# One kernel, one change: undivided softmax weights go through the turn, and the product with the values is divided by VectorE

## The reference, cut to what matters

```python
keys = modulated_linear(x, s, ...)      # [batch, position, 256]
# 16 heads of 16 features; for each batch and position the 16 heads attend to each other
w = softmax(q @ k.T * 16 ** -0.5)       # over the 16 heads j
o = w @ v                               # product with the values
x = x + modulated_linear(o, s, ...)
```

## Time and profile before

| | |
|---|---|
| median of 3 runs | 538.26 us (537.77 to 538.40) |
| span of the profiled execution | 537.6 us; its own time is not given apart, the median lies 0.7 us above the span |
| PE matmuls busy | 462.3 us, 86% |
| VectorE busy | 347.5 us, 65% |
| ScalarE busy | 282.6 us, 53% |
| GpSimd busy | 170.1 us, 32% |
| mean granted TensorE clock | 0.926 |
| chain that ended last | PE 67%, VectorE 14%, issue 5%, DMA 5%, SP queue 4%, ScalarE 3%, GpSimd 2% |

### The profile page before, as it was taken

How to read it: one execution, slowest core, us unless ns; L and a number is a source line. 1 busy time by engine, 2 the same in 40 slices (tenths; PEclk the granted TensorE clock), 3 DMA queues, 4 the chain that set the end, 5 groups by cost and what they waited for, 6 DMA issues and landing times.

```text
span 537.6 us, 9360 instructions
## 1 busy us (share of the span) xinstructions
PE 462.3 (86%) x3768; PEld 259.2 (48%) x3768; DVE 347.5 (65%) x653; ACT 282.6 (53%) x421; POOL 170.1 (32%) x146
## 2 busy tenths in 40 slices
PE   3896668924899999999999999999999898849981
PEld 3673335512365546554555654565546555424431
DVE  0374547593387488749856983898388778454923
ACT  0201488262853976578756966793976497102100
POOL 3009895110304232413231323314231420172121
PEclk9998767986599999999999999999999999879986
DMA  5991700331733713553183338143713561320011
GB/s 152 341 265 57 193 1 21 92 97 52 186 97 84 231 57 106 160 154 88 76 215 99 119 81 212 69 157 69 207 41 122 139 166 54 101 78 19 0 40 39
DMA packets 68736, 61.00 MB, mean 113 GB/s; under 512 B 53910, under 2 KB 55572, under 8 KB 68308
## 3 DMA queue, kind: packets, MB, share of 16 engines
q1 hardware_dynamic: 64404, 43.86, 30.0%
q0 software_dynamic: 3712, 12.59, 7.4%
q10 hardware_dynamic: 576, 3.95, 2.0%
HBM read 39.18 MB, written 21.07 MB: 112 GB/s over the span
## 4 chain that ended last, share of the span: by engine, by line
PE 67%; DVE 14%; issue 5%; DMA 5%; SPq 4%; ACT 3%; POOL 2%; POOLq 0%; DVEq 0%; ACTq 0%
PE ph L750 17%; PE pk L729 10%; PE pp L712 5%; PE ph L712 4%; PE ph L838 3%; PE pp L759 3%; PE pp L871 2%; PE pp L854 2%; DVE kx L1621 2%; PE pp L810 2%; PE pk L720 2%; PE pk L648 1%; PE ph L648 1%; PE pk L750 1%; DMA bd<-in_w_dec 1%
## 5 line engine op out<-in xcount | busy, mean ns | idle before, releaser
L1140 ACT ACTIVATE bd<-vc,ownrow 128x512 f32<-128x512 f32 x124 | 78.3, 711 | 0.0
L1127 ACT ACTIVATE bd<-kc,ownrow 128x512 f32<-128x512 f32 x120 | 75.6, 709 | 0.3
L447 POOL TENSOR_TENSOR demod<-demod,neghalf 128x32 f32<-128x32 f32 x8 | 43.4, 5448 | 35.2 <-DVE demod L1382 35.2
L729 PEld LDWEIGHTS pk<-bd,kc 128*32 128x32 f32 x1024 | 30.4, 120 | 17.1 <-issue 11.7
L729 PE MATMUL pk<-bd,kc 128*32 128x128 f32 x1024 | 35.4, 298 | 3.2 <-ACT bd L1127 3.2
L485 POOL TENSOR_TENSOR attnT<-attnT,style 128x1024 f32<-128x1024 f32 x6 | 11.4, 1901 | 76.4 <-DMA attnT<-av_dram 76.4
L712 PE MATMUL pp<-ys,kwT 128*128 128x512 f32 x64 | 30.6, 623 | 2.6 <-DVE ys L1604 2.6
L729 PE MATMUL pk<-bd,et 128*32 128x128 f32 x1024 | 31.1, 273 | 0.0
L729 PEld LDWEIGHTS pk<-bd,et 128*32 128x32 f32 x1024 | 27.2, 110 | 3.6 <-issue 3.2
L750 PE MATMUL ph<-tT,w 128*128 128x512 f32 x56 | 27.3, 633 | 0.1
L750 PE MATMUL ph<-x2T,w 128*128 128x512 f32 x56 | 25.9, 605 | 1.2 <-DVE h L1698 1.2
(11 more groups left out here) (348 smaller groups left out, 976.3 us busy)
## 6 DMA issues: line engine op xcount, KB each, us to landing
xin<-in_x SPq DMA_DIRECT2D x8, 512.0 KB, 4.5
x_dram<-x SPq DMA_DIRECT2D x8, 512.0 KB, 2.6
k_dram<-kxb SPq DMA_DIRECT2D x16, 256.0 KB, 3.3
kt<-k_dram SPq DMA_DIRECT2D x8, 512.0 KB, 4.0
v_dram<-kxb SPq DMA_DIRECT2D x8, 512.0 KB, 5.0
vt<-v_dram SPq DMA_DIRECT2D x8, 512.0 KB, 5.8
x1r<-x_dram SPq DMA_DIRECT2D x8, 512.0 KB, 3.5
av_dram<-av SPq DMA_DIRECT2D x8, 512.0 KB, 5.8
```

Of the source, the lines that this page charges most:

```text
L447: gp.tensor_tensor(q, q, neghalf[:, 0:4 * CB].rearrange("p (l a b) -> p l a b", l=2, a=2), ALU.pow).then_inc(gs_dem, 1)
L729: ins = mm(pk[32 * r:32 * r + 32, o:o + 128], weights(h, 4 * i + r)[:, 16 * pair:16 * pair + 32], bd[:, h, 8 * i + 2 * r + pair, :], start ...
L1127: fn(bd[:, h, :, 16 * b:16 * b + 16].rearrange("p (q z) x -> p q z x", z=2), kc[:, 16 * h:16 * h + 16, :].rearrange("p q (z x) -> p q z x" ...
L1140: fn(bd[:, h, :, 16 * b:16 * b + 16], vc[:, SH * h:SH * h + SH, :], ACT.Copy, scale=ownrow[:, 1, b:b + 1]).then_inc(s, 1)
```

## The change

The exponential (step 3) now writes straight to `osb` in the order (i, j, b), and PE turns these undivided weights without waiting for VectorE: its wait is for `a_ex0` or `a_ex1` instead of `v_p0` or `v_p1`. The wait for the turn back of the chunk before (`p_back0`, `p_back1`) moves with it from VectorE to ScalarE. `quotients` sums from `osb`, takes the reciprocal and no longer multiplies. The copy of the product (step 8) leaves ScalarE: VectorE multiplies the bank of the product by `rz` and writes `osb`. 16 multiplies and 16 copies go, 16 multiplies from PSUM come. In a middle turn the one of half 0 stands on VectorE where the multiply of half 1 stood, and the one of half 1 behind the aggregates of `h` and ahead of `xnT`. In `step_v7` there are three: the one of half 1 of chunk 6 at the latter place, the one of half 0 of chunk 7 behind the reciprocal of half 1, and the one of half 1 of chunk 7 between `yn` and the moments of `xin`.

```diff
@@ PE, every place of the kind
-                    after(pe, v_p1, d)
+                    after(pe, a_ex1, d)
                     quarter_turns(1, p_eT1)
...
-                    after(pe, a_osb0, d)
+                    after(pe, v_osb0, d)
                     quarter_turns(0, p_back0)
@@ ScalarE
-            def outputs_out(h, s):
-                fn(osb[:, h, :].rearrange("p (i d b) -> p i d b", i=4, b=CB),
-                   pk[:, 512 * h:512 * h + 512].rearrange("p (i b d) -> p i d b", i=4, b=CB), ACT.Copy).then_inc(s, 1)
+            def exponentials(h, s):
+                fn(osb[:, h, :].rearrange("p (i j b) -> p i b j", i=4, b=CB),
+                   es[:, h, :].rearrange("p (i b j) -> p i b j", i=4, b=CB), ACT.Exp, scale=SCALE).then_inc(s, 1)
...
-                    fn(es[:, 1, :], es[:, 1, :], ACT.Exp, scale=SCALE).then_inc(a_ex1, 1)
+                    after(act, p_back1, v - 1)
+                    exponentials(1, a_ex1)
                     after(act, p_s1, v)
                     value_blocks(1, 0, 4, a_bv1)
-                    after(act, p_av0, v)
-                    outputs_out(0, a_osb0)
                     value_blocks(1, 4, 8, a_bv1)
@@ VectorE
-            def quotients(h, c, s_sum, s_rz, s_p):
-
-                w = es[:, h, :].rearrange("p (q j) -> p q j", j=NH)
-                ve_.reduce_sum(zs[:, h, :], w, AX.X).then_inc(s_sum, 1)
+            def quotients(h, c, s_sum, s_rz):
+
+                ve_.reduce_sum(zs[:, h, :], osb[:, h, :].rearrange("p (i j b) -> p i b j", i=4, b=CB), AX.X).then_inc(s_sum, 1)
                 after(ve_, s_sum, c)
                 ve_.reciprocal(rz[:, h, :], zs[:, h, :]).then_inc(s_rz, 1)
+
+            def outputs_out(h, c, p_av, p_eT, s_rz, s):
+
+                after(ve_, p_av, c)
+                after(ve_, p_eT, c)
                 after(ve_, s_rz, c)
-                tt(osb[:, h, :].rearrange("p (i j b) -> p i b j", i=4, b=CB),
-                   es[:, h, :].rearrange("p (i b j) -> p i b j", i=4, b=CB),
-                   rz[:, h, :].rearrange("p (i b) -> p i b", b=CB).unsqueeze(3).to_broadcast([128, 4, CB, NH]), ALU.mult
-                   ).then_inc(s_p, 1)
+                tt(osb[:, h, :].rearrange("p (i d b) -> p i b d", i=4, b=CB),
+                   pk[:, 512 * h:512 * h + 512].rearrange("p (i b d) -> p i b d", i=4, b=CB),
+                   rz[:, h, :].rearrange("p (i b) -> p i b", b=CB).unsqueeze(3).to_broadcast([128, 4, CB, HD]), ALU.mult
+                   ).then_inc(s, 1)
@@ VectorE, step, behind the aggregates of h
+                if d is not None:
+                    outputs_out(1, d, p_av1, p_eT1, v_rz1, v_osb1)
+                if e is not None:
                     after(ve_, p_sg, e)
                     tt(xnT[:, :, :], xnT[:, :, :], halves(P23), ALU.mult).then_inc(v_sT, 1)
@@ VectorE, step_v7
                 after(ve_, a_ex1, v)
-                after(ve_, p_back1, v - 1)
-                quotients(1, v, v_sum1, v_rz1, v_p1)
+                quotients(1, v, v_sum1, v_rz1)
+                outputs_out(0, v, p_av0, p_eT0, v_rz0, v_osb0)
                 after(ve_, p_y, e)
...
                     stt(yn[:, j, :], y[:, j, :], mv[:, 2, j, 0:1], last_gb[:, 0, :], ALU.subtract, ALU.mult).then_inc(v_yn, 1)
+                outputs_out(1, v, p_av1, p_eT1, v_rz1, v_osb1)
                 after(ve_, a_x2k, d)
```

54 lines of the change are left out of this document (24 added, 30 removed).

## The result

Four runs of the kernel before gave 537.77 to 538.40 us (median 538.26); the changed kernel gave 544.72 to 549.17 us in three runs (median 547.84), 1.6% more (ratio 1.0161, 95% interval 1.0117 to 1.0205). The forecast was 547.1. A second series (experiment 11) gave 542.0 to 549.8 us in six runs, median 547.1. Ratios and medians leave out disturbed executions, but the profiled ones of experiments 2, 5, 7, 8 and 10 are such, with a first turn of 68 to 71 us instead of 48 to 50, so all times of the drain are counted from PE's turn of `h` at its head.

The account below looks back on a forecast made before the run. PE has no room in middle turns, and the drain's end follows `xn`. Terms -0.3 + 0 + 0.2 + 0.5 + 2.1 + 1.8 + 5.2 - 0.7 = +8.8 on 538.3 gave 547.1 us, range 543.4 to 550.4.

Parts of the forecast that it names:

- Prices: Changed operations: exponential 1.03 us (bounds 0.63 and 1.08), sum 1.08, multiply from PSUM 1.09.
- Part 1: Start, second turn: VectorE loses a multiply, exponential and sum get slower; -0.3 us, between -0.8 and 0.
- Part 2: Third turn: PE's next list entry 0.8 us late against the gained start, absorbed by the wait for `attnT`; 0.
- Part 3: Middle turns: the new multiply makes `h` ready just as PE takes it, a draw; +0.2 us in all.
- the sign that I gave: Forecast wrong if middle turns lengthen by 0.3 us or more, or `xin` moments begin less than 6 us later.
- Part 4: Head of the drain: the multiply finds 0.48 us of idle time while PE waits for `h`; +0.5 us.
- Part 5: End of the drain: first product's wait +2.1 us, half clock for `hidden(4)` +1.8, second product's wait +5.2.
- Part 6: End of the drain: store of y lands faster because `av`'s store starts later; -0.7 us, between -2.5 and 0.
- The waits alone: Rival: no low clock in PE's new gap, store shrinks to 3.4 us; 543.5 us, chance 0.18.
- Middle turns lose: Rival: multiply from PSUM costs 1.5 us or more, or the clock falls at the drain's head; 550.3 us, chance 0.17.
- ScalarE's freed time: Rival: in `step_v7` ScalarE copies x2 earlier, so moments of `xin` begin 1.5 us earlier; 536.5 us, chance 0.03.
- Absorbed: Rival: something other than `xn` ended the drain and covers the 9 us; no change, chance 0.02.

Follow-up runs that it names:

- experiment 11: The changed kernel run once more, unaltered, in a second series: 547.1 us, ratio 1.0134.
- experiment 2: Changed kernel with VectorE's division of half 1 in `step_v7` moved behind the last operation on y, after `xn`: 538.1 us, ratio 1.0001.
- experiment 5: Changed kernel with `values(1)` ahead of `hidden(4)` on PE in `step_v7`, VectorE's order untouched: 540.8 us, ratio 1.0039.
- experiment 7: Changed kernel with exponential, sum and division in plain element order, for timing only: 547.9 us, ratio 1.0203.
- experiment 8: Kernel before, with y's last operation ahead of the moments of `xin` and its store ahead of their rstd: 535.0 us, ratio 0.9938.
- experiment 10: Kernel of experiment 9, with ScalarE's copy of the turned `xn` ahead of the outputs of half 1: 533.9 us, ratio 0.9904.
- experiment 1: Kernel before, with only two waits added on VectorE for `values(0)` and `values(1)` in `step_v7`: 542.2 us, ratio 1.0088.
- experiment 9: Changed kernel reordered in `step_v7`: `values(1)` before `hidden(4)`, both divisions behind the moments of `xin`, `gtm` copy and store early: 534.5 us, ratio 0.9940.
- experiment 3: Changed kernel with the division of half 0 in `step_v7` behind `yn`, its turn back behind `hidden(4)`: 541.0 us, ratio 1.0050.
- experiment 4: Changed kernel with the turn back of half 0 in `step_v7` issued five times to fill PE's gap: 546.1 us, ratio 1.0139.
- experiment 6: Changed kernel with the division of half 1 issued twice in the five middle turns: 552.6 us, ratio 1.0286.

## Why the prediction was right

**Prices.** Exponential 1.145 us (1.03 predicted), sum 1.077 (1.08), division 1.043 (1.09). The exponential lies above the upper bound of 1.08 that I gave it; experiment 7 shows that it hardly mattered.

**Part 1, -0.3.** Not readable: up to the turn of `xin` of the third turn the profiled executions with an ordinary first turn took 101.8 to 105.3 us whatever the kernel (104.8 before, 101.8 after, 104.1 in experiment 1, 102.6 in 9). Neither shown nor refuted. My lower end of -0.8 was wrong too: without the two slowdowns all of PE's 1.05 us of idle time could be won, and the "0.4 us lower" in the paragraph on prices should have been up to 0.75.

**Part 2, 0.** Right in experiments 2 to 6, 9 and 10: the third turn is 60.7 to 61.0 us there, and 60.84 and 60.78 in experiments 1 and 8, which have the old code in it. Not so in the two profiled executions of the changed kernel itself (63.17 and 62.62), and why is open (experiment 11). In detail PE's entry behind `shift` came 29.86 us into the turn against 28.91: 0.95 us late (0.8 forecast); in the experiments that is absorbed ahead of `attnT`.

**Part 3, +0.2.** The sum is 0.5, but spread otherwise. Three of four turns kept 50.55 us and one took 51.05. PE and VectorE there:

```profile
326.13 1.09 PE L759 MATMUL pp<-ident,h 128*128 128x128 f32 x8 [0.28 <-DVE h L1507]
```
```profile
322.15 1.08 DVE L1459 TENSOR_TENSOR osb<-pk,rz 128x512 f32<-128x512 f32 x1
323.07 1.21 DVE L1504 TENSOR_TENSOR xnT<-xnT,pp 128x1024 f32<-128x1024 f32 x1
324.20 1.87 DVE L1507 TENSOR_SCALAR h<-h,mv,rstd 128x256 f32<-128x256 f32 x4
```

In that turn `h` took 1.87 us instead of the 1.37 of the others, where it is ready 0.45 us before PE takes it. "A draw" was nearly the right reading; I had `h` at the 1.68 us of the earlier trace rows. The same turn is 51.03 to 51.05 us long in experiments 2 to 5 and 9 to 11, 50.56 with the shorter operations of experiment 7 and 50.55 to 50.60 with the old code (before, 1 and 8), so the half microsecond belongs to the change. By the sign that I gave, 0.3 us a turn, one turn fails and the mean, 0.12 us, does not.

**Part 4, +0.5.** Wrong by its size: PE waits 1.47 us for `h`, as against 1.42. The division moved what follows it by 0.9 us, found 0.48 idle, and `h` itself was done in 1.38 us instead of 1.68.

**Part 5, +2.1, +1.8 and +5.2.** The term that decides, and right in its places: +2.06, +2.73 and +5.11. The second was undersized. I took eight matmuls at 5.37 us from the earlier trace rows, and in the new gap they took 6.43 us. Experiment 1 shows how near this was to nothing: idle for 2.39 us, clock 1.00. The moments of `xin` began 9.9 us later against the head of the drain, well beyond the 6 us of my sign. One of the signs was off: VectorE waited 8.44 us for the second product and not about 5. By my own sum it should have been some 7.4 (`yn` done at 456.2, `values(1)` at 459.7 + 2.1 + 1.8), and the clock adds 0.9.

**Part 6, the store, -0.7.** Undersized too, on the other side: the store landed in 3.70 us instead of 5.89, -2.19, close to the far end that I named. The mechanism is the one forecast (last section): the turns of `xn` and of half 1 took 1.97 and 1.06 us instead of 1.09 and 0.60, and `av`'s store started 1.72 us behind `out`'s instead of 0.43. Only "shares the queues" was wrong, since the profile has `out`'s store in q0 and `av`'s in q1; what both use is the 16 DMA engines, whose share is 0.97 to 1.08 from 464 to 467 us. The gain could not have been larger: `h` no longer waits, because VectorE's `tT` ended 0.1 us after the landing. The errors of parts 4, 5 and 6 (-0.5, +0.8 and -1.5 us) largely cancel with +0.3 in part 3 and +0.55 behind `h`, which I had not counted, and so do the start's -3.0 and the third turn's +2.65; that is why 547.1 lay so near. The runs of the changed kernel spread over 4 to 8 us in either series, so a distance of 0.7 us says nothing by itself. The base adds a little: in each of the later profiled executions its own time is 1.74 to 1.84 us above its span, so the profile of before was, as an estimate, some 1.1 us slower than the median to which I added. The mechanism is right; the nearness is partly chance.

**The rivals.** *The waits alone* lacked the clock's drop, which came in all five profiled executions with a gap of 2.8 us or more. *Middle turns lose* is out at 0.5 us. *ScalarE's freed time* is out in this order, and the reason that I gave (`values(1)` comes behind `hidden(4)`) is what experiment 5 turned round. *Absorbed* is out.

## What to carry to other kernels

When an operation moves to an engine that works in order, look first at what stands behind it there, not at its price: two waits without any work cost 3.8 us, and 1.3 us of longer operations cost nearly nothing. Ask next whether the awaited work can be put earlier on its own engine, or the waiting one into a wait that exists already (rstd here). Then follow the chain on to the next stop; a gain or a loss ends at whichever comes last, here a store whose buffer the next step writes.
